# V's bias added to the context by ScalarE in every group, instead of once through the output projection

## What is computed

```python
q = split(hidden_states @ Wq.T + bq)
k = split(hidden_states @ Wk.T + bk)
v = split(hidden_states @ Wv.T + bv)
...
probs = jax.nn.softmax(scores, axis=-1)
ctx = jnp.einsum('bhst,bhtd->bhsd', probs, v)
ctx = ctx.transpose(0, 2, 1, 3).reshape(Bn, t, D)
return ctx @ Wo.T + bo
```

## Time and profile before

| | us |
|---|---|
| median of 3 runs | 546.66 |
| lowest and highest run | 546.57, 546.98 |
| the profiled execution, its time | 546.76 |
| its span in the profile | 545.0 |
| its granted TensorE clock | 1.00 in all 40 slices |

### The profile page before, as it was taken

The page is one execution under the profiler, slowest core; times in us unless marked ns, Lnnn a source line. Parts: engine busy times, 40 slices in busy tenths (PEclk is TensorE's granted clock), DMA queues, the critical chain, the costliest instruction groups (busy, mean ns, idle before and its releaser), DMA issues.

```text
span 545.0 us, 10146 instructions
## 1 busy us (share of the span) xinstructions
PE 538.2 (99%) x3936; PEld 424.2 (78%) x3936; DVE 375.1 (69%) x717; ACT 283.1 (52%) x510; POOL 290.3 (53%) x262
## 2 busy tenths in 40 slices
PE   8999999999999999999999999999999999999997
PEld 7877888878888888888888888766686667866676
DVE  6999886888665886659898987355944668344422
ACT  5857886977767786776653442034501344023310
POOL 5398798985783657877795348034400343013320
PEclk9999999999999999999999999999999999999999
DMA  8951222273215310239563712100071001600001
GB/s 291 342 212 65 77 81 78 79 228 123 75 44 161 111 59 2 79 109 299 187 238 101 266 32 103 41 1 0 0 155 38 1 0 27 149 20 0 1 20 59
DMA packets 56176, 53.91 MB, mean 99 GB/s; under 512 B 15168, under 2 KB 37952, under 8 KB 56128
## 3 DMA queue, kind: packets, MB, share of 16 engines
q1 hardware_dynamic: 56128, 53.25, 31.0%
HBM read 36.46 MB, written 13.63 MB: 92 GB/s over the span
## 4 chain that ended last, share of the span: by engine, by line
PE 82%; POOL 10%; DVE 5%; issue 2%; ACT 0%; POOLq 0%; DVEq 0%
PE bank L312 33%; PE bank L506 24%; PE bank L526 15%; POOL q_w L828 2%; POOL q_w L826 2%; POOL probs L819 2%; POOL x_res L842 2%; PE bank L307 2%; PE bank L440 2%; PE bank L450 1%; PE bank L409 1%; DVE q_m L1363 1%; PE bank L361 1%; PE bank L537 1%; PE bank L556 1%
## 5 line engine op out<-in xcount | busy, mean ns | idle before, releaser
L312 PE MATMUL bank<-reduced 128*128 128x512 f32 x936 | 223.3, 394 | 0.3 <-DVE ctxT L1307 0.3
L312 PEld LDWEIGHTS bank<-reduced 128*128 128x128 f32 x936 | 172.8, 188 | 38.2 <-issue 1.1
L934 POOL TENSOR_TENSOR f_parts<-fused,f_parts 128x512 fp32r<-128x512 f32 x48 | 62.9, 1310 | 154.3 <-ACT f_parts L1206 154.3
L1188 ACT ACTIVATE tanh_g<-bank,half_gate 128x512 f32<-128x512 f32 x48 | 33.0, 687 | 141.8 <-PE bank L506 133.0
L526 PE MATMUL bank<-reduced,f_parts 128*128 128x512 f32 x360 | 83.5, 392 | 0.0
L526 PEld LDWEIGHTS bank<-reduced,f_parts 128*128 128x128 f32 x360 | 67.4, 188 | 14.2
L506 PE MATMUL bank<-reduced 128*128 128x512 f32 x288 | 72.1, 402 | 0.0
L1552 DVE SCALAR_TENSOR_TENSOR silu<-tanh_g,bank 128x512 f32<-128x512 f32 x48 | 32.9, 685 | 56.8 <-ACT tanh_g L1188 56.8
L506 PEld LDWEIGHTS bank<-reduced 128*128 128x128 f32 x288 | 54.1, 188 | 12.9
L826 POOL TENSOR_TENSOR q_w<-q_w,q_m 128x512 f32<-128x512 f32 x36 | 49.7, 1381 | 7.8 <-DVE q_m L1365 7.8
L819 POOL TENSOR_SCALAR_AFFINE_SELECT probs<-probs 128x1024 f32<-128x1024 f32 x32 | 37.0, 1161 | 31.0 <-ACT probs L1001 31.0
(11 more groups left out here) (135 smaller groups left out, 761.9 us busy)
## 6 DMA issues: line engine op xcount, KB each, us to landing
quantized<-q_w SPq DMA_DIRECT2D x36, 256.0 KB, 3.4
reduced<-quantized SPq DMA_DIRECT2D x12, 512.0 KB, 6.8
memT_sb<-in_memT SPq DMA_DIRECT2D x16, 256.0 KB, 4.9
mem_sb<-in_mem SPq DMA_DIRECT2D x16, 256.0 KB, 5.9
out<-y_sb SPq DMA_DIRECT2D x15, 256.0 KB, 2.1
q_w<-in_gate_w SPq DMA_DIRECT2D x12, 256.0 KB, 3.5
q_w<-in_up_w SPq DMA_DIRECT2D x12, 256.0 KB, 3.2
x_res<-in_x SPq DMA_DIRECT2D x3, 1024.0 KB, 8.9
```

Of the source, the lines that this page charges most:

```text
L312: ins = pe.matmul(dst, stationary, moving, start=(n == 0), stop=(n == len(pairs) - 1))
L934: pool.tensor_tensor(f_lo[:, f, :], fused[:, f % 2, :], f_hi[:, f, :].bitcast(F32), ALU.subtract).then_inc(f_lo_ready, 1)
```

## The change

ScalarE adds `bv_c[:, hg]`, one value per partition, to `ctxT` in place (an Identity activation with a bias read from SBUF), waits for that with the new semaphore `ctx_biased`, and then makes the rounded copy as before. This happens in all 16 head groups. `bias_through`, `bias_out` and VectorE's four operations on `bv` and `Wo` are gone; `add_bo` waits for the load of `bo` instead. In groups 1 to 3 `context_high(g, 1)` now stands behind the four `x_high` (the high parts of the transposed x of the next group) and no longer between the second and the third; in group 0 it stays where it was.

```diff
@@ tensor
-            def bias_through():
-                dst, done = take(("BO",), PT_BANK)
-                pe.wait_ge(bv_step, KT)
-                pe.matmul(dst[:], ones[:], ctxT[:], start=True, stop=True).then_inc(done, 1)
...
                 for i in range(GT):
                     v_proj(g, i, (C_BANK, E_BANK, Q_BANK, K_BANK)[i])
-                    if g == 0 and i == 2:
-                        bias_through()
@@ gpsimd, add_bo
                 if g == 0:
-                    wait_drained(pool, ("BO",))
+                    pool.wait_ge(bo_loaded, 16)
@@ scalar, context_high
                 wait_drained(act, ("C", g, hg))
+
+                act.activation(ctxT[:], ctxT[:], ACT.Identity, bias=bv_c[:, hg:hg + 1]).then_inc(ctx_biased, 1)
+                act.wait_ge(ctx_biased, g * HG + hg + 1)
                 act.activation(cT_hi[:, hg, :], ctxT[:], ACT.Copy).then_inc(ctx_hi, 1)
@@ scalar, head group 2
                 for i in range(GT):
-                    if i == 2:
+                    if g == 0 and i == 2:
                         context_high(g, 1)
                     x_high(g + 1, i)
+                if g:
+                    context_high(g, 1)
@@ vector
-            def bias_out():
-                src = wait_filled(dve, ("BO",))
-                dve.wait_ge(bo_loaded, 16)
-                dve.tensor_tensor(bo_b[:], src[:], bo_b[:], ALU.add).then_inc(drain_sem(("BO",)), 1)
...
-            for k in range(KT):
-                rows = raw[3][:, k * D:(k + 1) * D]
-                if k == 0:
-                    dve.wait_ge(raw_loaded[WO_PART], 16)
-                    dve.tensor_scalar(ctxT[:], rows, bv_c[:, k:k + 1], None, ALU.mult).then_inc(bv_step, 1)
-                else:
-                    dve.wait_ge(bv_step, k)
-                    dve.scalar_tensor_tensor(ctxT[:], rows, bv_c[:, k:k + 1], ctxT[:], ALU.mult, ALU.add)\
-                        .then_inc(bv_step, 1)
...
                     if g == 0:
                         weight_low(WO_PART)
-                        bias_out()
```

More of the change, by code:

```diff
@@ L235, in build @@
         bo_added = sem("bo_added")
-        shift_step, shift_made, bv_step = sem("shift_step"), sem("shift_made"), sem("bv_step")
+        shift_step, shift_made, ctx_biased = sem("shift_step"), sem("shift_made"), sem("ctx_biased")
         memT_loaded = [sem(f"memT_loaded{n}") for n in range(GT)]
```

## The result

| | before | after |
|---|---|---|
| median of 9 runs, us | 546.67 | 548.32 |
| lowest and highest run | 546.51, 547.12 | 547.90, 548.92 |
| the profiled execution, its time | 546.76 | 547.90 |
| its span in the profile | 545.0 | 546.2 |

The changed kernel takes 1.003 times as long, with a 95% interval from 1.0022 to 1.0039: **slower by 0.3%, some 1.65 us**. The profiled executions differ by less, 1.14 us. Part of the reason is chance: TensorE's first products for the scores (`bias_r`, L398 before) began at 15.27 us and not at 15.67, ahead of every changed instruction, so that this execution has a start of 0.40 us that has nothing to do with the change; it is also the shortest of its nine. In the twelve profiles of this document these products begin between 15.27 and 15.72, in no order of what was changed.

A forecast was written before the change was run, and what follows sets the result against it. TensorE, busy 538.2 of 545.0 us, was taken as the bound. Terms -0.93 + 0.72 - 0.4 + 0.72 + 0.5 + 0.6 = +1.2 on the profiled 546.76 gave 547.97, median 0.10 below: 547.9 us, range 545.9 to 549.2.

The forecast's parts named there:

- removal of `bias_through`: On TensorE before the context at 34.52: the removed instruction costs 0.93 us with nothing beside it, so -0.93.
- place 1: (0, 1) to (0, 2): GpSimd's gapless work delays the mask, +0.72, less 0.4 for fewer collisions; TensorE then at -0.6.
- place 2: (0, 3) to (1, 2): the GpSimd and VectorE slab chain passes its later start to its end, +0.72; TensorE at +0.1.
- place 3: First cross-attention step of group 2: delayed `mem_lo` makes `x_pT_lo` 0.72 later against 0.24 of margin, +0.5.
- place 4: First cross-attention step of group 3: same delay as in group 2, with a margin of 0.12, +0.6.
- later: After the cross-attention steps: the feed-forward part keeps its length, so nothing is added.
- ScalarE's step: Each head group: biased Identity 0.69 us plus 0.03 semaphore wait, rounded copy 0.72 later; mostly covered by ScalarE's idle time.
- The rival by which the collisions in it grow or go: GpSimd and VectorE collisions: gone in both early stretches, 545.6 us, chance 0.12; grown in the 49 us chain, 549.2, chance 0.13.
- The move: Groups 1 to 3: low part about 1.3 us later, hidden behind GpSimd's gap in (g, 3); cost 0, uncovered 0.3 per group.
- The lock falls the other way: Cross-attention: `mem_lo` no longer held by GpSimd's slab instruction, saving 0.97 us; both cross-attention terms vanish, 546.8; chance 0.35.
- The signs that had been named: TensorE busy about 1 us less, context(1, 2) waiting over 1, half-us waits at first `mem_hi` products of groups 2 and 3.
- term 1 or 2: The terms up to context(0, 2) and context(1, 2); wrong if these come earlier than 53.4 or 113.0.

The follow-up runs named there:

- i2: h with the changed kernel's two ScalarE activations (bias in place, then copy) and a plain subtraction on VectorE for the low part: 546.87 us.
- e4: The changed kernel without the bias activation at (1, 2) and (2, 2), right before the cross-attention steps: 546.87 us.
- e5: e4 with context_high(1, 1) back between the x_high of group 1: 546.47 us.
- e2: The changed kernel with context_high(g, 1) back between the second and third x_high in groups 1 to 3: 549.02 us.
- g: The changed kernel with the bias added in place by VectorE instead of ScalarE, and context_high not moved: 547.01 us.
- h: The changed kernel with the bias inside the rounded copy, low part one VectorE operation instead of GpSimd's, context_high not moved: 545.14 us.
- i1: The kernel before with only the low part put on VectorE, bias still through the output projection: 546.31 us.
- e1: The changed kernel without its bias activations and without the move of context_high, so V's bias is left out: 545.24 us.

## Why the prediction was right, and where its terms were off

The forecast was 547.9 with a range of 545.9 to 549.2. The time was 548.32, on the side that had been given the largest chance, by 0.45 against 0.43 for no change. The terms, each against the trace (which started 0.40 us early, so the start is taken out; the row of place 1 contains the removal, and the sum counts it once):

| term | predicted | in the trace |
|---|---|---|
| removal of `bias_through` | -0.93 | -0.91 |
| place 1, as far as TensorE at (0, 2) | -0.6 with it | -0.91 with it |
| place 2, (0, 2) to (1, 2) | +0.72 | +0.68 |
| place 3, group 2 | +0.5 | +1.35 |
| place 4, group 3 | +0.6 | +0.87 |
| later | 0 | -0.47 |
| sum | +1.2 | +1.5 |

- **The removal** is right, by the view that it rested on: -0.91 from the first `bias_r` products to context(0, 0).
- **ScalarE's step** was put at 0.69 + 0.03; it took 0.72 + 0.03. The nearest row, K's bias out of PSUM, was 0.03 too short for a source in SBUF. The Trainium skill (ScalarE: Activation LUTs, "What ACT_TABLE_LOAD costs") gives 280 ns + 0.833 ns per element, an estimate of 706 ns, which is nearer: the median of the 16 is 714. By it the sum would have been under 0.1 us higher, and closer.
- **Place 1** has the mechanism that was forecast. GpSimd's start moved by -0.63, which is -0.23 without the early start, as against -0.21. The collisions that left the stretch were worth 0.67, the end of the 0 to 0.7 that had been given for them, and not 0.4. That is the whole of the 0.3 by which the term was off.
- **Place 2** holds to a few hundredths. A chain of 49 us in which two engines feed each other kept its length (48.87 and 48.80), so the delay at its head came out at its tail. The rival by which the collisions in it grow or go fell.
- **Place 3** is where the working failed. The step "ScalarE's next wait for TensorE is only 0.17 us, so 0.55 of the delay reaches `mem_hi`" followed one path, by way of `mem_lo` to `x_pT_lo`, and took the margin of its last reader, 0.24. The change also makes the tanhs of scores(2, 0) late, and these free the banks that the first `cross` products write. That reader had no place in the working: PEld waits 0.52 and 0.34 there, TensorE loses 0.70 from context(1, 2) on before it reaches the product that was watched. And the delay was more than 0.72, since ScalarE waited 0.76 for `x_bias`, held up behind the norm. By i2 the step alone, with no work of GpSimd across the norm and `mem_lo`, costs nothing here.
- **The move** was put at 0, with GpSimd's gap in (g, 3) as its cover. GpSimd's work is indeed covered. What was not asked is what it falls upon: VectorE's norm, which went from 3.51 to 5.50 us. By e4 and e5 the move costs 0.3 us of the step in group 2, and by e2 as much. The sentence "in exchange `x_high` isn't delayed by the bias" was left without a number; by e2 the exchange is worth more, and without the move the kernel takes 0.7 us longer.
- **Place 4** has the same two losses as group 2, the one for the banks being smaller: 0.17 for them and 0.61 up to the product, which waited 0.42 for `x_pT_lo`; 0.87 in all, for 0.6.
- **Later**, 0.47 comes back. Before, VectorE's four slab operations at 255.85 took 1.27, 1.40, 0.41 and 1.38 us beside GpSimd's, and TensorE waited 0.32 at 267.13. In the changed kernel the same four find GpSimd idle, and the wait at that place is gone. That the one is the cause of the other is read from the two traces and was not tried. The timeline of VectorE there, the first and the last of the four:

```profile
259.69 0.42 DVE L1354 TENSOR_SCALAR q_m<-q_w 128x512 uint32<-128x512 uint32 x1
...
260.94 0.43 DVE L1356 TENSOR_SCALAR q_m<-q_m 128x512 f32<-128x512 f32 x1
```

- **The lock falls the other way** was the strongest rival, with 0.35. It did not: in the changed kernel GpSimd's slab instruction again starts first, at 132.27, and `mem_lo` from 132.34 is held until it ends, 134.11 against 133.56. As had been argued against the rival, both engines are shifted alike, and the phase stays; in group 3 it is the same (199.93 and 200.01). The rival's price doesn't hold in general: in g `mem_lo` isn't held, and the two steps cost 0.89 and 0.83 all the same; in i2 it isn't held, and they cost 0.01 and 0.04.
- **The signs that had been named.** The waits at the first `mem_hi` products of groups 2 and 3 came, with 0.41 and 0.42. TensorE's busy time fell by 0.2 and not by 1. context(0, 2) and context(1, 2) came at 53.08 and 112.91, earlier than the 53.4 and 113.0 from which term 1 or 2 was to be wrong. Without the early start they stand at 53.48 and 113.31, inside by less than a tenth and by 0.3: term 1 was off by 0.3, term 2 was not. The wait at context(1, 2) was 0.62 and not over 1, since part of it is taken at 91.11. The lower end of the range, 545.9, is 0.2 below what its working gives, 546.8 - 0.7.

The errors were of 0.3 (collisions gone) and 0.5 (later) on one side and 0.85 and 0.27 (cross-attention) on the other. The sum is nearer than its parts; the right sign in the end came by the places, the right size in part by luck. What stays open is the rest between the profiled executions and the medians in the changed kernel, 0.1 us once the early start is taken off.

## What to carry to other kernels

If one engine is at 99%, work given to an engine that is half idle is free only where nobody waits for what stands behind it. For each delayed instruction, list everyone who reads its result or takes the buffer that it frees, not only the reader on the path one has in mind; here a tanh that empties a bank was as dear as the operand. An addition is cheapest as an operand of an instruction that is there anyway: as part of the rounded copy (with the low part on VectorE) the bias cost ScalarE 0.09 us per tile and left a kernel 0.3% faster than before; as an activation of its own it cost more than it saved, and 1.7 us more with the low part in the same place (i2).

## What the hardware did that was not expected

- **How far GpSimd stretches VectorE.** The same four operations (128x512, fp32, SBUF to SBUF) took 1.91 us alone (h, i1 and i2), 3.51 before and in e1, 4.38 in e5, 5.46 in e4 and 5.50 in the changed kernel, by what GpSimd did beside them: up to 2.9 times as long. GpSimd's own instructions took 1.27 to 1.48 us there, at most 0.2 longer. The Trainium skill (SBUF — State Buffer, "SBUF: two separate sides") tells of the shared ports as a lock that is held for a whole instruction; the rows agree, and add that with GpSimd's instructions back to back each of VectorE's waits for one of them.
- **The end of a held operation.** `mem_lo` ended 0.55 us after the GpSimd instruction that held it (134.11 and 133.56); before it was 0.54 (133.11 and 132.57). Alone it takes 0.68 (h, 129.61). So it does almost all of its work after the other has ended, whatever its start in the record says.
- **Busy time is not work.** VectorE lost five instructions and was busy 5.2 us more. In e1, with the same five gone and nothing added, it was busy 370.2 us, 10.1 less than in the changed kernel, which has no VectorE instruction more.
